# A six-layer graph attention stack on one core: a new order of the work around layer 0's result, and layer 5's context as three products of high and low halves

## The reference

```
layer 0:  q, k, v = x@Wq+bq, x@Wk+bk, x@Wv+bv        # 8 heads
          h = softmax(mask(q@k.T * 32**-0.5)) @ v     # per head
          x = layer_norm(x + h@Wo + bo) * gamma + beta
layer 1:  x = layer_norm(x + softmax(mask(x@Wq @ (x@Wk).T / 16)) @ (x@Wv) @ Wo + bo) * gamma + beta
layers 2..5:
          q, k = x@Wq.T + bq, x@Wk.T + bk             # 128 wide
          x = layer_norm(x + softmax(mask(q@k.T / sqrt(128))) @ x @ Wc.T) * gamma + beta
```

## Time and profile before

| | |
|---|---|
| median of three runs | 2340.16 us |
| the profiled execution: its own time, its span | 2338.19 us, 2336.4 us |
| TensorE busy | 2257.7 us, 97%, 20624 instructions |
| TensorE weight loads | 2132.9 us, 91% |
| VectorE busy | 1771.6 us, 76%, 7736 instructions |
| ScalarE busy | 1614.4 us, 69%, 5515 instructions |
| GpSimd busy | 1787.6 us, 77%, 2397 instructions |
| mean granted TensorE clock | 0.994 of full |
| chain of waits by engine | PE 78%, DVE 9%, ACT 8%, issue 2%, POOL 2% |

### The profile page before, as it was taken

How to read it: one execution, slowest core, us unless ns; L and a number is a source line. 1 busy time by engine, 2 the same in 40 slices (tenths; PEclk the granted TensorE clock), 3 DMA queues, 4 the chain that set the end, 5 groups by cost and what they waited for, 6 DMA issues and landing times.

```text
span 2336.4 us, 59698 instructions
## 1 busy us (share of the span) xinstructions
PE 2257.7 (97%) x20624; PEld 2132.9 (91%) x20624; DVE 1771.6 (76%) x7736; ACT 1614.4 (69%) x5515; POOL 1787.6 (77%) x2397
## 2 busy tenths in 40 slices
PE   6899999999999999999999999999999999999986
PEld 5799999999999999999999999999999999999985
DVE  4777877877877877777777777777778778777776
ACT  5667767767767767767767767767677677677653
POOL 3368878878878878878788788788788788788762
PEclk9999999999999999999999999999999999999998
DMA  4000110110110110010010100100100100000000
GB/s 157 20 24 24 31 29 24 31 29 24 31 29 24 30 30 24 27 33 22 29 31 24 28 29 26 29 28 27 28 29 26 29 27 28 29 25 26 11 15 14
DMA packets 38747, 68.78 MB, mean 29 GB/s; under 512 B 4400, under 2 KB 12848, under 8 KB 37936
## 3 DMA queue, kind: packets, MB, share of 16 engines
q1 hardware_dynamic: 38448, 64.97, 9.2%
HBM read 48.18 MB, written 16.78 MB: 28 GB/s over the span
## 4 chain that ended last, share of the span: by engine, by line
PE 78%; DVE 9%; ACT 8%; issue 2%; POOL 2%; DMA 0%; POOLq 0%; SPq 0%; DVEq 0%
PE value_bank L464 17%; PE qk_bank L456 16%; PE context_bank L619 9%; PE unit_bank L464 8%; PE unit_bank L456 7%; PE score_bank L603 5%; PE qk_bank L569 5%; ACT probs L740 5%; PE unit_bank L523 5%; PE unit_bank L535 3%; PE score_bank L600 2%; DVE scores L919 2%; PE score_bank L610 2%; DVE xT_lo L948 2%; DVE scores L954 1%
## 5 line engine op out<-in xcount | busy, mean ns | idle before, releaser
L1190 POOL TENSOR_TENSOR x<-y,rows 128x512 f32<-128x512 f32 x304 | 390.3, 1284 | 188.5 <-DVE y L1007 188.5
L740 ACT ACTIVATE probs<-scores,negmax 128x128 f32<-128x128 f32 x1024 | 400.8, 400 | 88.9 <-DVE negmax L919 88.9
L1007 DVE TENSOR_SCALAR y<-y,mv,rstd 128x256 f32<-128x256 f32 x728 | 299.4, 453 | 175.7 <-POOL rstd L1174 175.5
L456 PE MATMUL qk_bank<-xT_hi,w_lo 128*128 128x256 f32 x1280 | 414.9, 324 | 17.0 <-DVE xT_lo L948 13.0
L1198 POOL TENSOR_TENSOR x<-x,rows 128x512 f32<-128x512 f32 x304 | 392.5, 1291 | 19.1
L762 ACT CAST xT_hi<-qk_bank 128x512 fp32r<-128x512 f32 x257 | 150.1, 584 | 355.0 <-PE qk_bank L569 354.9
L464 PE MATMUL value_bank<-w_lo,xT_hi 128*128 128x256 f32 x1280 | 393.7, 308 | 0.0
L456 PE MATMUL qk_bank<-xT_lo,w_hi 128*128 128x256 f32 x1280 | 362.5, 283 | 0.0
L456 PE MATMUL qk_bank<-xT_hi,w_hi 128*128 128x256 f32 x1280 | 360.8, 282 | 0.0
L464 PE MATMUL value_bank<-w_hi,xT_lo 128*128 128x256 f32 x1280 | 360.8, 282 | 0.0
L464 PE MATMUL value_bank<-w_hi,xT_hi 128*128 128x256 f32 x1280 | 358.8, 280 | 0.0
(11 more groups left out here) (98 smaller groups left out, 6532.7 us busy)
## 6 DMA issues: line engine op xcount, KB each, us to landing
x0T<-xT_in SPq DMA_DIRECT2D x64, 256.0 KB, 3.0
x<-x_in SPq DMA_DIRECT2D x64, 256.0 KB, 3.1
out<-x_out SPq DMA_DIRECT2D x64, 256.0 KB, 2.3
adj<-adj_in SPq DMA_DIRECT2D x64, 128.0 KB, 2.2
late_weights<-w_in SPq DMA_DIRECT2D x2, 1024.0 KB, 7.3
rows<-rows_in SPq DMA_DIRECT2D x1, 1792.0 KB, 11.6
probs0T<-w_in SPq DMA_DIRECT2D x4, 256.0 KB, 4.1
x<-w_in SPq DMA_DIRECT2D x1, 1024.0 KB, 13.1
```

The costliest lines, as they stand in the source:

```text
L456: mm = pe.matmul(psum[:, n * G * N:(n + 1) * G * N], split(w, name, kd, at, at + P), flat(xT_half[:, kd]), start=kd == 0 and w is w_lo, st ...
L740: e = act.activation(probs0[:, j, g, quad], scores0[:, j, g, quad], ACT.Exp, scale=-1.0, bias=negmax0[:, j, g, quad:quad + 1], accum_out=t ...
L1007: m = dve.tensor_scalar(y[:, r, g], y[:, r, g], mv[:, r, g, 0:1], rstd[:, r, g:g + 1], ALU.subtract, ALU.mult)
L1190: pool.tensor_tensor(result(norm), y[:, NORM_AT[norm] % YS], row_of_each(f"gamma{layer}"), ALU.mult).then_inc(zg_ready, 1)
```

## The change

Two things are changed.

*The order around layer 0's result.* On VectorE, in slot 3, the residual and statistics of layer 0 now stand ahead of the normalisation of layer 5's item. In slots 4 and 0 the low half of x (and in slot 4 the normalisation of layer 0) now stand ahead of the row maximum of the item before. On GpSimd, in slot 3, the deviation of layer 0 now stands ahead of layer 5's `scale`. On ScalarE the exponentials `exp0(group, 0)`, four in slot 4, are cut: those of the first graph stay in slot 4, those of the second stand in slot 0, behind `split_hi`.

*Layer 5's context.* For the first 60 groups ScalarE moves `v` and `probsT` of layer 5 out of PSUM as float32r high halves (same shape as the copies before), VectorE computes both low halves (one instruction of 128x512 and one of 128x256, both in slot 2), and the context is three float32r products for each graph, six instead of four matmul instructions in an item. Who waited for a moved value or a moved probability matrix waits, behind a layer 5 item, for its low half. `move_v` also waits for the context two items before.

```diff
+def in_halves(i):
+    return item(i)[0] == LAYERS - 1 and i < LAST_FIRST
...
             def context(i):
-                pe.wait_ge(probsT_ready, after(i))
-                pe.wait_ge(v_ready, after(i))
+                wait_probsT_moved(i)
+                wait_values_moved(i)
...
                 for g in range(G):
-                    mm = pe.matmul(context_bank[:, g * D:(g + 1) * D], probsT[:, ring(i), g], v[:, ring(i), g],
-                                   start=True, stop=True)
+                    if not in_halves(i):
+                        mm = pe.matmul(context_bank[:, g * D:(g + 1) * D], probsT[:, ring(i), g], v[:, ring(i), g],
+                                       start=True, stop=True)
+                        continue
+                    for left, right in ((probsT_hi, v_lo), (probsT_hi, v_hi), (probsT_lo, v_hi)):
+                        mm = pe.matmul(context_bank[:, g * D:(g + 1) * D], left[:, ring(i), g], right[:, ring(i), g],
+                                       start=right is v_lo, stop=left is probsT_lo)
...
@@ ScalarE @@
             for i in LOOP_SLOTS:
                 if item(i):
                     split_hi(i)
+                if (group := due(i, 5)) is not None and item(i - 1):
+                    exp0(group, 0, [1])
...
                 if (group := due(i, 6)) is not None:
-                    exp0(group, 0)
+                    exp0(group, 0, [0] if item(i) else range(G))
...
+            def split_v(i):
+                dve.wait_ge(v_hi_ready, IN_HALVES_AT[i] + 1)
+                dve.tensor_tensor(flat(v_lo[:, ring(i)]), value_bank[:, :], flat(v_hi[:, ring(i)]).bitcast(F32),
+                                  ALU.subtract).then_inc(v_lo_ready, 1)
...
@@ VectorE @@
             for i in LOOP_SLOTS:
-                if item(i - 1):
+                urgent = due(i, 1) is not None or due(i, 0) is not None
+                if item(i - 1) and not urgent:
                     row_max(i - 1)
                 if item(i):
                     split_lo(i)
                 if (group := due(i, 1)) is not None:
                     finish_or_normalise(("group", group))
+                if item(i - 1) and urgent:
+                    row_max(i - 1)
                 if (group := due(i, 2)) is not None:
                     split_headsT(group)
+                if item(i - 1) and in_halves(i - 1):
+                    split_v(i - 1)
...
-                if item(i - 2):
-                    finish_or_normalise(("item", i - 2))
                 if (group := due(i, 2)) is not None:
                     add_residual(("group", group))
                     statistics(("group", group))
+                if item(i - 2):
+                    finish_or_normalise(("item", i - 2))
+                if item(i - 1) and in_halves(i - 1):
+                    split_probsT(i - 1)
...
@@ GpSimd @@
                 if item(i - 1):
                     keep_valid(i - 1)
+                if (group := due(i, 2)) is not None:
+                    find_rstd(("group", group))
                 if item(i - 2):
                     scale(("item", i - 2))
...
                 if (group := due(i, 2)) is not None:
-                    find_rstd(("group", group))
                     scale(("group", group))
                     shift(("group", group))
```

More of the change, by code:

```diff
@@ L150 @@
 LATER_LEAD = 3
+def in_halves(i):
+    return item(i)[0] == LAYERS - 1 and i < LAST_FIRST
+IN_HALVES_AT = {i: at for at, i in enumerate(i for i in ITEMS if in_halves(i))}
+IN_FULL_AT = {i: at for at, i in enumerate(i for i in ITEMS if not in_halves(i))}
 KEPT = [i for i in ITEMS if item(i)[0] > 1]
@@ L215, in gnn_stack @@
         v = sb("v", [RING, G, D])
+        v_hi = sb("v_hi", [RING, G, D], F32R)
+        v_lo = sb("v_lo", [RING, G, D], F32R)
+        probsT_hi = sb("probsT_hi", [RING, G, N], F32R)
+        probsT_lo = sb("probsT_lo", [RING, G, N], F32R)
         scores = sb("scores", [RING, G, N])
@@ L293, in gnn_stack @@
         v_ready = sem("v_ready")
+        v_hi_ready = sem("v_hi_ready")
+        v_lo_ready = sem("v_lo_ready")
         scores_in_psum = sem("scores_in_psum")
@@ L581, in project_qk, with wait_values_moved, wait_probsT_moved @@
                 project(qk_bank, xT_hi[:, ring(i)], xT_lo[:, ring(i)], parts).then_inc(qk_in_psum, 1)
+            def wait_values_moved(i):
+                if in_halves(i):
+                    pe.wait_ge(v_lo_ready, IN_HALVES_AT[i] + 1)
+                else:
+                    pe.wait_ge(v_ready, IN_FULL_AT[i] + 1)
+            def wait_probsT_moved(i):
+                if in_halves(i):
+                    pe.wait_ge(probsT_lo_ready, IN_HALVES_AT[i] + 1)
+                else:
+                    pe.wait_ge(probsT_ready, IN_FULL_AT[i] + 1)
             def project_v(i, g):
@@ L734, in move_k0, with exp0 @@
                 m.then_inc(k0_ready, 1)
-            def exp0(group, j):
+            def exp0(group, j, graphs=range(G)):
                 act.wait_ge(negmax0_ready, after_unit(group, j))
-                for g in range(G):
+                for g in graphs:
                     for quad in range(QUADS):
@@ L782, in move_v @@
                 act.wait_ge(v_in_psum, after(i))
-                act.copy(flat(v[:, ring(i)]), value_bank[:, :]).then_inc(v_ready, 1)
+                if NTH[i] >= RING:
+                    act.wait_ge(context_in_psum, after(i) - RING)
+                if in_halves(i):
+                    act.copy(flat(v_hi[:, ring(i)]), value_bank[:, :]).then_inc(v_hi_ready, 1)
+                else:
+                    act.copy(flat(v[:, ring(i)]), value_bank[:, :]).then_inc(v_ready, 1)
             def softmax(i):
@@ L793, in move_probsT @@
                 act.wait_ge(probsT_in_psum, after(i))
-                act.copy(flat(probsT[:, ring(i)]), score_bank[:, 0:G * N]).then_inc(probsT_ready, 1)
+                if in_halves(i):
+                    act.copy(flat(probsT_hi[:, ring(i)]), score_bank[:, 0:G * N]).then_inc(probsT_hi_ready, 1)
+                else:
+                    act.copy(flat(probsT[:, ring(i)]), score_bank[:, 0:G * N]).then_inc(probsT_ready, 1)
             def split_first(name):
@@ L965, in move_v1, with split_probsT @@
                                   ALU.add).then_inc(v_ready, 1)
+            def split_v(i):
+                dve.wait_ge(v_hi_ready, IN_HALVES_AT[i] + 1)
+                dve.tensor_tensor(flat(v_lo[:, ring(i)]), value_bank[:, :], flat(v_hi[:, ring(i)]).bitcast(F32),
+                                  ALU.subtract).then_inc(v_lo_ready, 1)
+            def split_probsT(i):
+                dve.wait_ge(probsT_hi_ready, IN_HALVES_AT[i] + 1)
+                dve.tensor_tensor(flat(probsT_lo[:, ring(i)]), score_bank[:, 0:G * N],
+                                  flat(probsT_hi[:, ring(i)]).bitcast(F32), ALU.subtract).then_inc(probsT_lo_ready, 1)
             def add_residual(norm):
```

9 lines of the change are left out of this document (6 added, 3 removed).

## The result

The changed kernel takes 2427.31 us (median of five runs, 2426.28 to 2432.87) against 2340.16 (2338.26 to 2341.12) beside it: a ratio of 1.0378, 95% interval 1.0363 to 1.0392. It is 87 us slower, 1.45 us in each of the 60 full periods. The profiled execution took 2426.52 us, its span 2424.7, at a mean granted TensorE clock of 0.995 (0.994 before), so the clock plays no part.

What follows compares the result with a forecast made beforehand. TensorE's own work (busy 97%) was taken as the floor, its weight loads' waits (90.6 us) as all an order could give. +1.54 - 0.15 = +1.39 us over 60 periods, +83 us, gave 2423 us; own range 2405 to 2440, eight in ten 2342 to 2436.

Steps and rivals of the forecast that it cites:

- the case with both meetings: Likeliest case, chance 0.45: VectorE normalisations collide with GpSimd in slots 4 and 1; +1.39 us a period, 2423 us.
- the first meeting: Slot 4: layer 0's normalisation on VectorE overlaps GpSimd's `scale` of layer 5; row maxima 0.55 us later.
- the second meeting: Slot 1: VectorE's normalisation meets GpSimd's second half of `normalise_probs0` and `shift`, ending at about 1204.4.
- the slack of 0.07: ScalarE chain from slot 0's softmax to slot 1's low half: a softmax later than 1197.09 is paid by TensorE.
- Context: Layer 5's context on TensorE: six float32r products in 0.71 us instead of 0.86, gaining 0.15 us a period.
- Slot 4: VectorE step: low half first, then layer 0's normalisation ending at 1192.20 instead of 1191.68; `row_max0` 0.55 us later.
- Slot 0: VectorE's low half (0.61 us) ahead of the row maximum; softmax moves from 1197.02 to 1198.06.
- the normalisation of slot 1: Layer 3's normalisation on VectorE ahead of slot 1's row maximum; foreseen to ask at 1202.45 and last near 1.9 us.
- Slot 1: Row maximum moves from 1202.86 to 1204.40, TensorE's projection +1.54 us; which `normalise_probs0` half is met has 0.12 us margin.
- The rival with one meeting: Slot 1's normalisation meets the first half of `normalise_probs0`, keeping 1.24 us: +0.82 us a period, 2389 us; chance 0.22.
- The rival without meetings: No port collisions in slots 4 and 1, only slot 0's low half counts: +0.32 us a period, 2359 us; chance 0.12.
- The faster rival: TensorE's waits for ScalarE and GpSimd go, 52.8 us, plus 9 us of context: 2278 us; chance 0.14.

Runs made afterwards that it cites:

- small_scale5: Changed kernel with GpSimd's `scale` for layer 5 cut to one column of each graph (gamma left out elsewhere): 2390.12 us.
- small_shift5: Changed kernel with GpSimd's `shift` for layer 5 cut to one column of each graph (beta left out elsewhere): 2400.2 us.
- after_max3_first: Changed kernel with `row_max0(group, 3)` put ahead of `reciprocal0(group, 1)` on VectorE in slot 0: 2398.88 us.
- halves_only: Changed kernel with all old orders put back, keeping only layer 5's new float32r context: 2329.0 us, 0.9962 of the kernel before.
- both_small5: Changed kernel with both GpSimd's `scale` and `shift` for layer 5 cut to one column of each graph: 2362.15 us.
- halves_exp: Kernel before plus layer 5's new context and the second half of `exp0(group, 0)` moved to slot 0: 2327.16 us.
- best_try: `halves_exp` with `exp0(group, 2)` behind slot 1's `split_hi`, low half before row maximum in slots 0 and 1, `row_max0(group, 3)` before `reciprocal0(group, 1)`: 2343.37 us.
- low1: `halves_exp` with `exp0(group, 2)` moved behind slot 1's `split_hi` and the low half ahead of the row maximum in slot 1 alone: 2317.64 us.

## Why the prediction was right

*The forecast.* 2423 us against 2427 measured, by the case with both meetings: 1.39 us a period foreseen, 1.45 found. Both kernels can be laid side by side at slot 4's transposes, 1189.20 before and 1195.16 now (TensorE, changed kernel):

```profile
1195.16 0.60 PE L587 MATMUL qk_bank<-eye,x 128*128 128x128 f32 x4
```

From there the softmax of slot 0 comes 1.24 us later than before, foreseen 1.04, and the row maximum of slot 1 1.62 us later, foreseen 1.54. Up to the softmax the sum was 0.20 too small: layer 0's residual starts 0.16 us after the instant foreseen (1193.72 - 5.96 = 1187.76 against 1187.60), GpSimd's `scale` 0.22 after. Behind the softmax it was 0.12 too large. So each step is there at about its size, but that the total is within 0.1 us is in part two errors that cancel. The runs price the steps singly: 0.62 us for the first meeting (`small_scale5`), 0.61 for the low half ahead of the row maximum, 0.45 for what of the second meeting is not hidden behind ScalarE's high half (`small_shift5`, `after_max3_first`). With the slack of 0.07 taken off, that is 1.61.

*Context.* 0.71 us foreseen, 0.70 found; a gain of 9 us foreseen, 9.0 in `halves_only`. The low half of `probsT` was taken as 0.4 us; the row of it has 0.42. VectorE's idle time of the earlier trace rows did hide both low halves: its timeline in slot 2, changed kernel, still ends in an idle 1.56 us ahead of slot 3's row maximum.

```profile
1186.81 0.42 DVE L1022 TENSOR_TENSOR probsT_lo<-score_bank,probsT_hi 128x256 fp32r<-128x256 f32 x1
...
1188.79 0.29 DVE L1002 CUSTOM_DVE_ANT_0 scores<-score_bank,mask 128x128 f32<-128x128 f32 x1 [1.56 <-PE score_bank L633]
```

*Slot 4.* The meeting of the normalisation with `scale` was foreseen as an end 0.47 us behind GpSimd's, from the tail's row, and that is what it is (1198.37 against 1197.90). The Trainium skill, page "SBUF — State Buffer", section "Who interferes with whom", says that a VectorE instruction in a 2-port mode and GpSimd take one pair of ports as an exclusive lock, and that the later one blocks fully. The three kernels with a short `scale` or `shift` agree: each pair goes back to 0.73 or 0.96 us with its own GpSimd instruction made short.

*Slot 0.* ScalarE idles 1.00 us ahead of the softmax, foreseen 1.1, before 0.87. Putting the row maximum back there gives 59 us, more than its 0.61 us x 60 = 37, because it also decides which half the normalisation of slot 1 meets (27 us in `small_shift5`; the two overlap a little).

*Slot 1.* This was the step with a margin of 0.12 us. The normalisation did meet the second half and the `shift` behind it: 1.91 us, foreseen near 1.9. The margin was thin but it repeated, for the reason given: GpSimd's pair starts 0.08 us after the reciprocal ends, and the normalisation asks 0.71 us after the pair starts, in 55 of 59 periods. The rival with one meeting stood and fell with it; `after_max3_first` comes near to its case, 2399 us against the 2389 it was priced at, and the 0.20 us missing ahead of the softmax is the difference. The rival without meetings is nearly what `both_small5` makes, 2362 us; it was priced at 2359, though a pair of 0.96 us is still left there.

*The faster rival* rested on the waits for `kT` and for layer 0's x. The first went (31.7 to 4.8 us) and `halves_exp` shows what that is worth alone: about 2 us (3.5 by the ratios), not 27, because the low half waits in its stead. The second grew to 27.0 us: layer 5's `scale`, now under layer 0's normalisation, makes it end late, and layer 0's x with it. That the deviation comes earlier doesn't help x when the normalisation that uses it meets 1.27 us of other work.

*Not foreseen.* The value projection of slot 0 waits for the copy of the values, 38.6 us. The prediction named ScalarE's chain as gapless and late, but looked only for `split_hi` at its end. In the changed kernel this wait probably cost nothing: TensorE starts slot 1's transposes at 1208.23, and ScalarE, without a gap, takes up their high half only at 1209.78. No run here tests that. In `best_try` this very wait decides. The prediction also took the sum of the weight loads' waits (90.6 us before) as all that a better order could give. No run passed that bound, but it is no measure of what an order does gain: edits that took 26, 18 and 49 us of one kind out of that list (`halves_exp`, `low1`, `best_try`) gained about 2 and 8 us and lost 17.

## What to carry to other kernels

Before an instruction is moved ahead, look at what the other engines do at its new time, not only at what waits for it: here a pair of VectorE normalisations that started 0.4 us after a long GpSimd instruction took 1.35 us instead of 0.74. In a software pipeline that turns in a ring, a wait in the list names its last owner only; take it away and find the next one in the timeline before counting the gain. Price each part of a bundle alone: here a gain of 9 us and a loss of 96 came in one change.

## What the runs showed of the hardware

- A pair of VectorE normalisations (0.74 us alone) that starts under one GpSimd multiplication of 128x512 takes 1.35. Where it asks under the first half of `normalise_probs0` it takes 1.24; under the second half, with `shift` right behind, 1.91. There VectorE gets one of its two instructions in between two of GpSimd, and the second waits for the whole of the next. Each held instruction ends 0.14 to 0.16 us after the GpSimd instruction that held it (1198.05 after 1197.90, 1209.23 after 1209.09, 1210.52 after 1210.36).
- Not every VectorE instruction is held: the row maxima of layer 0 (one input from a bank) keep their length under that same GpSimd pair of 1207.90 to 1209.09. VectorE's timeline, changed kernel:

```profile
1207.97 0.29 DVE L967 CUSTOM_DVE_ANT_0 scores<-unit_bank,mask 128x128 f32<-128x128 f32 x1
...
1208.40 0.28 DVE L967 CUSTOM_DVE_ANT_0 scores<-unit_bank,mask 128x128 f32<-128x128 f32 x1
```

- Six float32r products of 128x256 take 0.70 us from start to start, the four float32 instructions that give the same two products 0.86.
